# Retention and mixture-of-experts layer on one core: down projections of three groups as three rounded products, the shared expert last in the last group

## What is computed

```python
def attn(x):                                  # x: normalised
    q, k = rotary(x @ Wq.T), rotary(x @ Wk.T)       # 4 heads of 32
    v, g = x @ Wv.T, x @ Wg.T                       # 4 heads of 64
    s = (q @ k.T) * 32**-0.5 * decay_mask           # per head, causal
    o = s @ v
    o = o / rms(o) * g_norm_w * silu(g)
    return o @ Wo.T
def ffn(x):                                   # x: normalised
    shared = silu(x @ sh_up_w + sh_up_b) @ sh_down_w + sh_down_b
    comb = top2_of_softmax(x @ gate_w.T)            # (tokens, 8), renormalised
    h = silu(x @ up_w[e] + up_b[e])                 # for e in 0..7
    y = sum_e comb[:, e] * (h[e] @ down_w[e] + down_b[e])
    return y + shared
x = x + attn(layernorm(x))
x = x + ffn(layernorm(x))
```

## Time and profile before

| | us |
|---|---|
| median of 3 runs | 136.29 (136.12 to 136.59) |
| the profiled execution, its own time | 136.48 |
| span of that execution, first to last instruction | 134.7 |
| PE busy | 128.8 (96%) |
| DVE busy | 102.9 (76%) |
| ACT busy | 81.2 (60%) |
| POOL busy | 43.6 (32%) |
| granted TensorE clock, mean | 0.997 |

### The profile page before, as it was taken

One profiled execution on the slowest core, in us unless ns is written; L12 is line 12 of the kernel. 1 busy time (PEld: TensorE's weight loads), 2 busy tenths in 40 slices (PEclk: granted clock), 3 DMA queues, 4 the chain that ended last, 5 costly groups with the idle time before them and its releaser, 6 DMA issues.

```text
span 134.7 us, 3595 instructions
## 1 busy us (share of the span) xinstructions
PE 128.8 (96%) x1359; PEld 101.7 (76%) x1359; DVE 102.9 (76%) x318; ACT 81.2 (60%) x146; POOL 43.6 (32%) x64
## 2 busy tenths in 40 slices
PE   5999899999999999999999999999999999999990
PEld 5897798999899988978665588566676557489980
DVE  3889999999999999995997728966249437425983
ACT  3359959677506369977848355977454834980230
POOL 6534599390707738264321107000004200000000
PEclk9999999999999999999999999999999999999998
DMA  4999900000000000009900593000961100002002
GB/s 108 290 372 336 335 24 0 5 0 7 5 0 5 0 5 0 2 12 287 339 1 5 146 403 136 21 0 27 324 277 40 42 2 0 0 15 65 5 0 78
DMA packets 8661, 12.53 MB, mean 93 GB/s; under 512 B 1298, under 2 KB 5676, under 8 KB 8644
## 3 DMA queue, kind: packets, MB, share of 16 engines
q1 hardware_dynamic: 8212, 11.84, 26.4%
q10 hardware_dynamic: 432, 0.46, 1.2%
HBM read 11.20 MB, written 1.10 MB: 91 GB/s over the span
## 4 chain that ended last, share of the span: by engine, by line
PE 81%; DVE 7%; ACT 4%; DMA 4%; issue 2%; ACTq 1%; DVEq 0%
PE bY L1281 16%; PE bU L1102 9%; PE bU L1104 8%; PE bU L1103 8%; PE bA L1178 6%; PE bA L1254 5%; DMA W<-wqkvg 4%; PE bU L1197 3%; PE bA L1146 2%; PE bA L1172 2%; PE bU L1138 2%; PE bY L1102 1%; PE bM L1215 1%; PE bM L1197 1%; PE bM L1217 1%
## 5 line engine op out<-in xcount | busy, mean ns | idle before, releaser
L509 ACT ACTIVATE HB<-bU,UB 128x512 f32<-128x512 f32 x36 | 24.6, 687 | 22.2 <-PE bU L1104 21.5
L884 DVE TENSOR_TENSOR HG<-CB,HB 128x512 f32<-128x512 f32 x24 | 16.9, 719 | 11.1 <-ACT HB L509 7.2
L1281 PE MATMUL bY<-HG,DW 128*128 128x512 f32 x48 | 24.6, 594 | 0.0
L1102 PE MATMUL bU<-XH,UWH 128*128 128x512 f32 x36 | 22.6, 628 | 0.2 <-ACT HB L509 0.2
L355 POOL TENSOR_TENSOR RR<-SS,NHALF 128x8 f32<-128x8 f32 x8 | 13.1, 1642 | 17.3 <-DVE SS L779 17.2
L1103 PE MATMUL bU<-XL,UWH 128*128 128x512 f32 x36 | 14.2, 395 | 0.0
L1104 PE MATMUL bU<-XH,UWL 128*128 128x512 f32 x36 | 14.2, 394 | 0.0
L369 POOL TENSOR_SCALAR VE<-MV 128x2 f32<-128x2 f32 x8 | 2.2, 281 | 29.2 <-DVE MV L804 29.2
L1102 PEld LDWEIGHTS bU<-XH,UWH 128*128 128x128 f32 x36 | 6.8, 189 | 5.4 <-issue 4.9
L760 DVE TENSOR_TENSOR SC<-bA,MASK 128x512 f32<-128x512 f32 x16 | 10.2, 680 | 0.1
L484 ACT ACTIVATE SQ<-bA 128x512 f32<-128x512 f32 x8 | 4.8, 598 | 8.9 <-PE bA L1178 8.9
(11 more groups left out here) (171 smaller groups left out, 312.3 us busy)
## 6 DMA issues: line engine op xcount, KB each, us to landing
CB<-scratch SPq DMA_DIRECT2D x12, 512.0 KB, 5.3
ROT<-rotary_tables SPq DMA_DIRECT2D x8, 256.0 KB, 4.7
out<-OUT SPq DMA_DIRECT2D x8, 128.0 KB, 1.8
X<-x SPq DMA_DIRECT2D x7, 128.0 KB, 4.7
UW<-upw SPq DMA_DIRECT2D x1, 576.0 KB, 4.8
DW<-dnw SPq DMA_DIRECT2D x1, 576.0 KB, 4.1
W<-wqkvg ACTq DMA_DIRECT2D x1, 256.0 KB, 4.9
W<-wqkvg ACTq DMA_DIRECT2D x1, 128.0 KB, 3.4
```

The lines of the kernel that those rows point to most:

```text
L509: act.activation(HB[:, k, :], bU[(g * (E + 1) + k) % 2][:, :], ACT.Silu, bias=UB[:, e:e + 1]).then_inc(hid.sem, 1)
L884: dve.tensor_tensor(HG[:, k % RING, :], CB[:, k - 1, :], HB[:, k, :], ALU.mult).then_inc(gated.sem, 1)
L1102: pe.matmul(out_, ah, bh, start=start, stop=False)
L1281: pe.matmul(bY[:, :], DW[:, e * P:(e + 1) * P], HB[:, 0, :] if k == 0 else HG[:, k % RING, :], start=(k == 0), stop=(k == E)).then_inc(dow ...
```

## The change

The nine down projections of groups 0, 1 and 2 (27 in all) become rounded products. For that the down weights are split at the start: ACT rounds `DW` to `DWH` (`split_down`), POOL makes the remainder `DWL` (`low_down`). For each of the 27 the second operand is split too: ACT rounds the gated hidden layer to `HGH` (`hi`), DVE subtracts for the remainder `HGL` (`lo`), and only then may PE start. In the last group the shared expert stands last (k = 8) and not first; its four products are added in `bY` and `bM` to the biases, and `final` adds the two halves to the weighted sum `YM` with one operation of 256 columns each. `base` is gone. `mix` starts from the residual and covers k = 0 to 7. To make room in memory, `HG` has 2 slots, `HGH` and `HGL` have 3, the pair buffers 3 instead of 4, the rotary tables 4 instead of 6, and `XN1`, `XN2` one buffer for a pair number instead of two, with waits for each. The orders of PE, DVE, ACT and POOL and the table `PLACE` are all written anew. The last store is started by ACT instead of SP.

```diff
-RING = 4
-SLOTS = 4
-TABLES = 6
+RING = 3
+SLOTS = 3
+TABLES = 4
...
-        def expert(k):
+        def expert(g, k):
+
+            if g == LAST:
+                return k
             return E if k == 0 else k - 1
...
+            def low_down():
+                pool.wait_ge(dw_hi.sem, 1)
+                pool.tensor_tensor(DWL[:, :], DW[:, :], DWH[:, :].bitcast(F32), ALU.subtract).then_inc(dw_lo.sem, 1)
...
+            def split_down():
+                act.wait_ge(ld_dn.sem, 16)
+                act.copy(DWH[:, :], DW[:, :]).then_inc(dw_hi.sem, 1)
+
+            def hi(g, k):
+                if k == 0:
+                    act.wait_ge(hid.sem, hid.at(g, 0))
+                else:
+                    act.wait_ge(gated.sem, gated.at(g, k - 1))
+                if k >= RING:
+                    act.wait_ge(down.sem, down.at(g, k - RING))
+                elif g:
+                    act.wait_ge(down.sem, down.at(g - 1, k + E + 1 - RING))
+                act.copy(HGH[:, k % RING, :], exact(k)).then_inc(g_hi.sem, 1)
...
-                if k > RING:
-                    dve.wait_ge(down.sem, down.at(g, k - RING))
+                if k > 2:
+                    wait_low(dve, g, k - 2)
                 elif g:
-                    dve.wait_ge(down.sem, down.at(g - 1, k + E - RING))
-                dve.tensor_tensor(HG[:, k % RING, :], CB[:, k - 1, :], HB[:, k, :], ALU.mult).then_inc(gated.sem, 1)
+                    wait_low(dve, g - 1, k + E - 2)
+                dve.tensor_tensor(HG[:, k % 2, :], CB[:, k - 1, :], HB[:, k, :], ALU.mult).then_inc(gated.sem, 1)
...
-            def base(g):
-
-                dve.wait_ge(biased.sem, 1)
-                dve.wait_ge(yt.sem, yt.at(g - 1))
-                dve.tensor_tensor(YS[:, :], bY[:, :], X[:, g * GC:(g + 1) * GC], ALU.add).then_inc(based.sem, 1)
+            def lo(g, k):
+                dve.wait_ge(g_hi.sem, g_hi.at(g, k))
+                dve.tensor_tensor(HGL[:, k % RING, :], exact(k), HGH[:, k % RING, :].bitcast(F32), ALU.subtract).then_inc(g_lo.sem, 1)
...
+            def final(g):
+
+                dve.wait_ge(stored[g - 2].sem, 32)
+                for h, src in enumerate((bY, bM)):
+                    if h == 0:
                         dve.wait_ge(last_half.sem, 1)
...
+                    dve.wait_ge(mixed.sem, TILES * (E - 1) + 2 * h + 2)
+                    dve.tensor_tensor(OUT[:, g % 2, 2 * h:2 * h + 2].rearrange("r m n -> r (m n)"), src[:, two(h)], YM[:, two(h)],
+                                      ALU.add).then_inc(tail.sem, 1)
...
-                pe.matmul(bY[:, :], DW[:, e * P:(e + 1) * P], HB[:, 0, :] if k == 0 else HG[:, k % RING, :], start=(k == 0),
-                          stop=(k == E)).then_inc(down.sem, 1)
+                w = slice(e * P, (e + 1) * P)
+                product(bY[:, :], (DWH[:, w], DWL[:, w]), (HGH[:, k % RING, :], HGL[:, k % RING, :]), k == 0,
+                        k == E).then_inc(down.sem, 1)
...
-            up_proj(3, 8)
-            down_last(3, 7)
-            down_last(3, 8)
+            up_proj(3, 8)
+            down_last(3, 7)
+            after(ct_sb, 3)
+            bias(3)
             down_last(3, 8)
```

More of the change, by code:

```diff
@@ new lines, in _ @@
+            qk_sb(3, 0)
+            hidden(0, 2)
+            comb_rows(0)
+            hi(0, 0)
+            hidden(0, 3)
+            comb_sb(0)
+            gates(3, 1)
+            x2_hi(1, 0)
+            hidden(0, 4)
+            squares(2, 1)
+            x2_hi(1, 1)
+            hidden(0, 5)
+            transposed_out(2, 0)
+            hi(0, 1)
+            hidden(0, 6)
+            qk_sb(3, 1)
+            hi(0, 2)
+            exps(1)
+            values(3, 0)
+            transposed_out(2, 1)
@@ new lines, in _ @@
+            rotate(3, 1)
+            gate_out(2, 1)
+            x2_lo(1, 1)
+            gating(0, 1)
+            gating(0, 2)
+            mean_squares(2, 1)
+            lo(0, 1)
+            route_a(1)
+            gating(0, 3)
+            rank(1)
+            lo(0, 2)
+            add_attention(2, 0)
+            gating(0, 4)
+            route_b(1)
+            stats2(2, 0)
+            add_attention(2, 1)
+            lo(0, 3)
+            stats2(2, 1)
+            gating(0, 5)
+            lo(0, 4)
@@ L1039, in _ @@
+            x2_bias(2, 0)
+            masked(3, 0)
+            gating(0, 6)
+            lo(0, 5)
+            x2_bias(2, 1)
+            state(3, 0)
+            gating(0, 7)
+            lo(0, 6)
+            gating(0, 8)
+            lo(0, 7)
+            x2_lo(2, 0)
+            gating(1, 1)
+            mean_squares(3, 0)
+            x2_lo(2, 1)
+            lo(0, 8)
+            lo(1, 0)
+            gating(1, 2)
             gate_out(3, 0)
-            gating(0, 8)
-            x2_lo(2, 0)
+            lo(1, 1)
@@ new lines, in _ @@
+            after(xl2, 0, 1)
+            out_t(1, 1)
+            after(qkt, 2, 1)
+            proj_g(3, 0)
+            attend(2, 0)
+            after(rparts, 3, 0)
+            proj_out(1, 1)
+            after(ogt, 1, 1)
+            up_proj(0, 0)
+            after(sg, 3, 0)
+            up_proj(0, 1)
+            after(x1, 1, 1)
+            qk_t(3, 0)
+            up_proj(0, 2)
+            after(route_a_step, 0, 0)
+            comb_t(0)
+            up_proj(0, 3)
+            after(hid, 0, 2)
@@ L1462, in _ @@
-            down_proj(0, 6)
-            after(ct_sb, 1)
-            x2_t(2, 0)
+            after(qkt, 3, 0)
+            proj_qk(3, 1)
+            after(sg, 3, 1)
+            up_proj(0, 4)
+            attend(2, 1)
+            after(hid, 0, 4)
+            x2_t(1, 1)
+            after(xl2, 1, 0)
+            up_proj(0, 5)
+            after(rparts, 3, 1)
+            down_proj(0, 0)
+            after(ct_sb, 0)
+            out_t(2, 0)
+            after(xl2, 1, 1)
+            up_proj(0, 6)
@@ new lines, in _ @@
+            after(hid, 0, 5)
+            qk_t(3, 1)
+            after(ogt, 2, 0)
+            router(1)
+            after(hid, 0, 6)
+            proj_out(2, 0)
+            after(qkt, 3, 1)
+            up_proj(0, 7)
+            down_proj(0, 1)
+            after(ogr, 2, 1)
+            proj_v(3, 0)
+            after(route_a_step, 1, 0)
+            out_t(2, 1)
+            down_proj(0, 2)
+            after(x1, 2, 0)
+            up_proj(0, 8)
+            proj_out(2, 1)
+            after(ogr, 2, 1)
@@ new lines, in _ @@
+            after(v_sb, 3, 0)
+            scores(3, 0)
+            after(hid, 0, 7)
+            proj_v(3, 1)
+            after(x1, 2, 1)
+            comb_t(1)
+            down_proj(0, 3)
+            after(v_sb, 3, 1)
+            up_proj(1, 0)
+            after(ct_sb, 1)
+            state_add(3, 0)
+            up_proj(1, 1)
+            down_proj(0, 4)
+            up_proj(1, 2)
+            after(hid, 1, 1)
+            x2_t(2, 0)
+            attend(3, 0)
+            down_proj(0, 5)
@@ L1497, in _ @@
+            after(x1, 3, 0)
+            comb_t(2)
+            up_proj(2, 1)
+            down_proj(1, 2)
+            up_proj(2, 2)
+            down_proj(1, 3)
+            after(hid, 2, 1)
+            out_t(3, 1)
+            down_proj(1, 4)
+            down_proj(1, 5)
+            after(ogt, 3, 1)
+            up_proj(2, 3)
             down_proj(1, 6)
-            up_proj(2, 1)
+            after(hid, 2, 2)
+            proj_out(3, 1)
             down_proj(1, 7)
-            up_proj(2, 2)
+            after(ct_sb, 2)
```

737 lines of the change are left out of this document (339 added, 398 removed), and 25 rows, old and new, of the table PLACE.

## The result

The changed kernel takes 137.66 us (median of 22 runs, 136.10 to 138.48), the kernel before, on the same chips, 136.56 (22 runs). The ratio, taken without the four slow runs (three of the changed kernel, one of before, each over 1.5% above the fastest of its kernel), is 1.0054, with a 95% interval of 1.0032 to 1.0075: slower by half a per cent, where 133.0 us and a gain of 2.4% were forecast. The profiled execution took 137.75 us, 1.27 more than that of before. The times of the changed kernel fall into two groups by the clock: six at 136.2 to 136.6 us, all with a mean granted clock of 1.000, and the rest at 0.983 to 0.988, fifteen of them at 137.5 to 138.5 us and one at 136.10; the profiled one is of the second group.

The account below looks back on a forecast made before the run. PE was taken as the bound, with DVE equally full up to 60 us. PE's work -4.2, tail -0.4 and PE waiting for DVE +1.3 gave -3.3 us, a median of 133.0 us, range 131.3 to 135.5.

Parts of the forecast that it names:

- PE's work: 27 down projections on PE as three rounded products each, 0.70 us instead of 0.86: 4.2 us less in all.
- tail: Behind PE's last products, DVE's new closing additions were to take 0.4 us less; the store stays.
- PE waits more: Between 46 and 113 us PE waits for late DVE: 1.3 us, taken between 0 and 2.0 plus handovers of about 0.5.
- POOL: The down weights' subtraction on POOL, 2.67 us ahead of the first `rms`, delays attention output: 0 to 0.5 us, taken 0.
- I see no reason for that to change: PE's clock, granted in full at 2.4 GHz, was to stay there as long as PE keeps as busy.
- a sign of being wrong: The first 46 us, whose order is new too, taking longer or shorter by more than 1 us.
- the 67 us over which DVE's load was spread: 46 to 113 us, where the down projections were expected: DVE's 48.6 us of work plus 16.2 added, 64.8.
- The variant of A: Full gain, with a rounded product on PE at 0.215 us: 6.2 us with the tail, 130.1; 20% together with A.
- DVE, ACT: Added work: 27 remainders on DVE at 0.60 us, 16.2 us; 27 copies on ACT, 14.6 us, and 1.2 for the weights.
- Rival B: Handovers between DVE, ACT and PE, 0.1 to 0.2 us in about 12 rounds, and exponentials eat most: 135.5 us, 20%.
- C: DVE becomes the bound, `lo` waiting for ACT's copy in all 27 rounds, 0.3 us exposed in each: 139.1 us, 7%.
- Rings: Waits for buffers with fewer slots, such as the three of `HGH`: no cost by themselves, 0.5 us at most.

Follow-up runs that it names:

- a_after_nm: The changed kernel with POOL's subtraction of 1152 columns waiting until DVE's 128x2 operation NM for pair (2,0) is done: 134.47 us, 0.9864 of before.
- d_two: The changed kernel with two small memsets ahead of POOL's 1152-column subtraction, NM in its old form with two tensor inputs: 138.12 us, 1.008 of before.
- d_one: The changed kernel with the same two memsets on POOL, and NM as two 128x1 operations with one tensor input each: 135.04 us, 0.9867 of before.
- c_short_lo: The kernel of a_after_nm with DVE's remainders computed for only 128 of 512 columns, the others zero: 133.12 us, 0.9764 of before.
- c_f32_down: The kernel of a_after_nm with the 27 down projections float32 again, all copies and remainders still made and waited for: 137.73 us.

## Why the prediction was wrong

The account goes from the profiled execution of before (span 134.7 us) to that of a_after_nm (132.7) and on to the changed kernel (136.0). PE's busy time from 9 us to its last product, and its idle time in between, come from the windows and the page: 121.4 busy and 0.9 idle before, 117.7 and 3.2 in a_after_nm, 119.1 and 5.1 in the changed kernel; from there to the end of the span 3.4, 2.8 and 2.8. How far an execution is at 13 us differs by up to 0.3 us among the three, so no term is surer than that.

| term | predicted | measured |
|---|---|---|
| PE's work | -4.2 | -3.7 |
| tail | -0.4 | -0.6 |
| PE waits more | +1.3 | +2.4 |
| sum without the hold | -3.3 | -1.9 |
| POOL's instruction | 0 | +1.9 idle, +1.4 clock |
| sum | -3.3 | +1.4 |

Without the hold the kernel takes 134.47 us, inside the stated range of 131.3 to 135.5 and 1.5 over the forecast; what put the changed kernel outside is the hold and the clock.

**The step that failed is "POOL".** I asked who waits for what stands behind the subtraction on POOL, and costed that at 0 to 0.5 us, taken 0 because DVE holds the pace there; a_after_nm confirms it, with a wait of 0.24. I didn't ask what DVE does while the subtraction runs, and DVE has no room for a hold there (busy 36.33 of 37 us). The row I took its price from, 2.67 us for the up weights, could not show the hold: in the kernel before, only DVE operations with an input in PSUM or with one input lay beside that instruction. But another place of the same trace did show one, and I had overlooked it. Three gatings in a row take 1.89 us; here two take 2.25, the second 1.43 instead of 0.69, beside POOL's multiplication of 512 columns:

```profile
83.05 1.04 POOL L362 TENSOR_TENSOR OG<-OGR,RR 128x512 f32<-128x512 f32 x1
...
82.39 2.25 DVE L884 TENSOR_TENSOR HG<-CB,HB 128x512 f32<-128x512 f32 x2
```

The Trainium skill (SBUF — State Buffer, "Who interferes with whom") says that a DVE instruction with two SBUF inputs contends with a GpSimd instruction that reads SBUF, that the ports the two share are an exclusive lock where the order of issue decides who blocks, and that an instruction with at most one such input outside the 2-port modes does not contend. The traces agree where POOL's instruction has 1152 columns: 2.59 us for d_two's NM, 0.33 for d_one's, and 2.90, 3.03 and 3.15 instead of 2.66 for POOL where it began 0.41, 0.53 and 0.63 us ahead of the end of a QKR (d_two, the changed kernel, d_one). Beside POOL's 1.66 us on 8 columns QKR passed, so the whole recorded length of a POOL instruction is not what blocks. This rule stood against the change, and I hadn't weighed it. With all 2.4 us of it on the path the sum would have been -3.3 + 2.4, before any word on the clock; 1.9 reached PE.

**"I see no reason for that to change" (the clock) failed with it.** It was tied to PE keeping busy, and PE didn't: 1.67 us of idle and then slow steps, 1.2 to 1.4 us, in 16 of 22 runs.

**PE's waits (1.3 forecast) are 2.4.** Between 60 and 113 us it is 1.28 against 0, in a_after_nm as in the changed kernel. The place was right, and the 1.3 agree partly by luck: two waits for remainders, 0.43 and 0.41, shrink to 0.13 and nothing in c_short_lo, but 0.39 for ACT's hidden layer stays, and that isn't DVE's lateness. What I hadn't priced is the stretch before: PE idles 1.4 us from 9 to 46 us in a_after_nm, 0.53 before, and 0.3 more from 46 to 60. It lies in waits of 0.5 and 0.6 us for ACT and DVE in the new order of the first steps (0.3 and 0.2 before); no run takes that order apart. In the changed kernel PE idles 3.28 us in the first 46, and more than 1 us there was named as a sign of being wrong. The down projections also run from 58.8 us on and not from 46, so the 67 us over which DVE's load was spread were 58.

**PE's work.** The step of 0.23 a product was right, but not 0.70 for every down projection. In a_after_nm's timeline 15 of the 27 take 0.69 to 0.71 us until the next product starts and the other 12 0.73 to 0.80, most of these directly behind a step of another form; together 19.6, 0.73 each. An estimate from that, 27 x (0.86 - 0.73), is 3.5, beside 3.7 measured and 4.2 forecast; c_f32_down costs 3.0. The variant of A with 0.215 a product is out.

**DVE, ACT.** 683 ns a remainder and 621 a copy, as the rows said; DVE waited for ACT's copies three times, 1.2 us in all, not 0.1 to 0.2 in each of 12 rounds. Rival B had the time nearly right for a kernel without the hold (135.5 against 134.47) but not by its mechanism, and C's, `lo` waiting in every round, doesn't occur. (C says that DVE would end 4.5 to 5 us before the old end; its own numbers give 132.4 - 127.1 = 5.3, which is what it then divides.) That the kernel is slower came from no rival. **Tail:** the last product to the end of DVE's work went from 1.15 to 0.48 us. **Rings:** ACT's copies waited 0.3 us for PE in all, which is the most that the three slots can have cost.

## What to carry to other kernels

When an operation is moved to or added on POOL, list the DVE operations that will run beside it, and look for those that read two tensors from SBUF: the size of the DVE operation doesn't matter, 128x2 was held for 2.4 us. Look in the trace that you have for operations of that form that are longer than their kind, since a mean hides them (719 ns over 24 gatings, one of them 1430). Start the long POOL instruction right behind the last such operation ahead of a stretch without them (one wait gave 3.2 us here), or give the DVE operation a form with one tensor input; cutting the instruction up bounds the hold, but cost 1.2 us of POOL (4.20 against 3.03). And a gap on PE of 1.7 us has to be costed with the slower products behind it, which were 1.2 to 1.4 us here in 16 of 22 runs.

## What the hardware showed that I had not expected

- A hold is recorded as busy time of the held instruction, without a wait in brackets: DVE's NM reads 2.59 us instead of 0.15, its stretch looks 100% busy, and the waits show up on ACT (2.67) and PE (1.67) only. The count of instructions in the window gives it away, 8 in 5 us (14 in a_after_nm).
- Which operation is caught changes with 0.1 us: QKR when POOL begins 0.09 us ahead of it, the NM behind it when POOL begins later.
- Rounded subtractions of 128 columns are recorded on POOL with 0.45 to 0.47 us each and start 0.42 apart (the first of the nine, which met a QKR, with 0.85); one of 1152 columns takes 2.66 us.
- Not every POOL instruction holds DVE: beside its 128x8 operation of 1.66 us a QKR took 0.69 us as ever.
